# Group norm statistics of the second batch taken inside the front stage instead of in the setup

## The reference, cut to what matters

```
def _gn(v, G=32, eps=1e-5):              # groups of 16 channels, over a whole batch
    g = v.reshape(B_, 32, 16, H_, W_)
    m = mean(g, axis=(2, 3, 4)); s = var(g, axis=(2, 3, 4))
    return (g - m) / sqrt(s + eps)

x = x + mamba_layer(_gn(x), ...)         # layer 0: per position a layer norm over the 512
                                         # channels, in_proj to 2048, a causal conv of 4 taps,
                                         # silu, x_proj, softplus, a selective scan, out_proj
x = x + codebook(_gn(x), m)              # layer 1: 1024 codes
```

## Time and profile before

| | |
|---|---|
| median of 3 runs | 4932.2 us (4929.79 to 4934.46) |
| profiled execution | 4925.77 us, its span 4924.1 us |
| PE busy | 4649.7 us (94% of the span) |
| DVE busy | 4135.4 us (84%) |
| POOL busy | 3377.7 us (69%) |
| ACT busy | 2971.5 us (60%) |
| setup, until the first chunk's load is issued | 0 to 66.4 us |
| group_params and preparation of chunk 0 | 66.4 to 95.3 us |
| front, 16 chunks | about 95 to 1130 us |

### The profile page before, as it was taken

How to read it: one execution, slowest core, us unless ns; L and a number is a source line. 1 busy time by engine, 2 the same in 40 slices (tenths; PEclk the granted TensorE clock), 3 DMA queues, 4 the chain that set the end, 5 groups by cost and what they waited for, 6 DMA issues and landing times. The chain is left out here.

```text
span 4924.1 us, 120048 instructions
## 1 busy us (share of the span) xinstructions
PE 4649.7 (94%) x47160; PEld 2945.8 (60%) x47160; DVE 4135.4 (84%) x4348; ACT 2971.5 (60%) x6008; POOL 3377.7 (69%) x1680
## 2 busy tenths in 40 slices
PE   4999999995899999999999999999999899999999
PEld 4666666663455555555555555555554688887787
DVE  7888898887999999999999999999997676776332
ACT  1666666665777767767777777777765454454111
POOL 0577776775999999999999999999997222222000
PEclk9999999997999999999999999999999999999999
DMA  5344334334223332333233323332332111111453
GB/s 201 120 154 150 141 134 150 142 145 163 85 77 96 96 97 79 96 97 96 79 96 99 98 84 96 95 98 79 96 98 76 44 76 77 77 77 75 190 201 139
DMA packets 191786, 538.37 MB, mean 109 GB/s; under 512 B 15824, under 2 KB 15840, under 8 KB 181840
## 3 DMA queue, kind: packets, MB, share of 16 engines
q1 hardware_dynamic: 185920, 480.31, 29.0%
q0 software_dynamic: 5104, 51.35, 2.7%
q10 hardware_dynamic: 288, 0.00, 0.0%
HBM read 329.22 MB, written 202.38 MB: 108 GB/s over the span
## 5 line engine op out<-in xcount | busy, mean ns | idle before, releaser
L975 POOL TENSOR_TENSOR sc_hc<-sc_hc,sc_c_rep 128x1024 f32<-128x1024 f32 x1024 | 2397.4, 2369 | 191.8 <-ACT sc_state L988 189.3
L1176 DVE TENSOR_TENSOR_SCAN sc_hc<-l_m,sc_state,sc_ring 128x512 f32<-128x512 f32 x2048 | 2432.0, 1259 | 32.5 <-PE sc_ring L1099 27.4
L1020 ACT ACTIVATE l_m<-l1s_v,l_neg_a 128x512 f32<-128x512 f32 x2048 | 1351.8, 707 | 2.5 <-issue 1.5
L1099 PEld LDWEIGHTS sc_ring<-sc_diag,l1s_iota 64*64 64x64 f32 x32768 | 890.6, 133 | 703.2 <-issue 703.2
L1099 PE MATMUL sc_ring<-sc_diag,l1s_iota 64*64 64x128 f32 x32768 | 1102.6, 275 | 8.0 <-DVE sc_hc L1176 5.7
L1109 PE MATMUL sc_y_ps<-sc_hc,sc_fold 128*64 128x512 f32 x4096 | 1008.4, 614 | 27.2 <-POOL sc_hc L975 20.9
L988 ACT ACTIVATE sc_state<-sc_hc 128x2 f32<-128x2 f32 x1024 | 206.0, 201 | 647.1 <-DVE sc_hc L1176 647.1
L851 PE MATMUL sc_o_ps<-l1s_et,l_sums 128*128 128x512 f32 x1024 | 560.6, 634 | 8.7 <-ACT l_count L841 8.7
L1431 POOL TENSOR_TENSOR l_count<-l_count,as_oh 128x1024 f32<-128x1024 f32 x64 | 182.4, 2851 | 506.9 <-DVE as_oh L1614 506.9
L1109 PEld LDWEIGHTS sc_y_ps<-sc_hc,sc_fold 128*64 128x64 f32 x4096 | 251.5, 137 | 415.9 <-issue 381.3
L71 PE MATMUL fr_mm<-fr_xn_hi,l0f_w_in_hi 128*128 128x512 f32 x1024 | 436.9, 427 | 26.3 <-DVE fr_delta L675 11.8
(11 more groups left out here) (172 smaller groups left out, 6518.4 us busy)
## 6 DMA issues: line engine op xcount, KB each, us to landing
sc_duz<-spill SPq DMA_DIRECT2D x128, 768.0 KB, 6.0
l1s_v<-spill SPq DMA_DIRECT2D x256, 256.0 KB, 3.9
spill<-fr_z SPq DMA_DIRECT2D x64, 512.0 KB, 2.8
spill<-fr_u SPq DMA_DIRECT2D x32, 1024.0 KB, 8.7
spill<-fr_du SPq DMA_DIRECT2D x32, 1024.0 KB, 4.3
spill<-fr_delta SPq DMA_DIRECT2D x32, 1024.0 KB, 6.4
sc_c_rep<-bc SPq DMA_DIRECT2D x128, 256.0 KB, 4.3
soft<-l1s_et SPq DMA_DIRECT2D x16, 2048.0 KB, 6.2
```

The source lines that it names most:

```text
L975: nc.gpsimd.tensor_tensor(hc[:, p], hc[:, p], c_rep[:, 2 * q:2 * q + 2, :], ALU.mult).then_inc(s_hp, 1)
L1020: nc.scalar.activation(da[:, p % 4, r, :], delta[:, i % 2, p % 2, :], ACT.Exp, scale=keep.neg_a[:, c:c + 1]).then_inc(s_da, 1)
L1099: done = nc.tensor.matmul(to[:, :, k::4], dut[rows, i % 2, k, HALF * h:HALF * h + HALF], diag[rows, u, 4 * q + c:4 * q + 4:2, k, :], start ...
L1176: nc.vector.tensor_tensor_scan(hc[:, p, r, :], da[:, p % 4, r, :], ring[:, SLOT[at], r::2], state[:, i, 2 * p + r:2 * p + r + 1], ALU.mult ...
```

## The change

`setup` loads and takes the statistics of the first batch's four tiles only (32 `bn_stats`). The weights come in two DMAs with a semaphore each; `lnw` and `lnb` are loaded by SP ahead of them. `group_params` between setup and front handles 4 columns instead of 8 (after the scan it handles 8 as before).

The second batch's 32 `bn_stats` run in chunks 0 to 6 of the front: SP loads a 1 MB chunk of x of the second batch into `sq`, once `sq` is free, and DVE takes 4 `bn_stats`, twice in chunk 0 (before conv 5 and before conv 7) and once in each of chunks 1 to 6 (before conv 7). In chunk 7, before the first chunk of the second batch is normalised, DVE aggregates (at the start of the chunk), PE does the two small matmuls (behind x1 and behind z1), ACT the Sqrt (behind its silu of z1), and DVE the operations between and the scale and shift (behind `rounded`, before `norm_v`).

```diff
@@ group_params
-    n = NB * KC
+    n = stats.shape[1]
@@ setup
         @block.sync
-            sp.dma_start(wf[:], d.w_in).then_inc(weights, 16)
-            with sp.Fori(0, NB * KC // 4) as i:
-                for s in range(4):
-                    sp.wait_ge(stats_done, 4 * i + s + 1)
-                    sp.dma_start(xt[:, s, :], x_rows[4 * i + s]).then_inc(x_tile[s], 16)
+            sp.dma_start(lnw[:], d.ln_w).then_inc(norm_w, 16)
+            sp.dma_start(lnb[:], d.ln_b).then_inc(norm_w, 16)
+            for k in range(2):
+                sp.dma_start(wf[:, 2 * k:2 * k + 2, :], d.w_in[:, 2 * k:2 * k + 2, :]).then_inc(weights[k], 16)
+            for k in range(KC):
+                sp.dma_start(xt[:, k, :], x_rows[k]).then_inc(x_tile[k], 16)
         @block.scalar
-            act.dma_start(lnw[:], d.ln_w).then_inc(norm_w, 16)
-            act.dma_start(lnb[:], d.ln_b).then_inc(norm_w, 16)
             act.wait_ge(norm_w, 32)
-            act.wait_ge(weights, 16)
             for k in range(KC):
+                act.wait_ge(weights[k // 2], 16)
...
         @block.tensor
-            pe.wait_ge(weights, 16)
+            for k in range(2):
+                pe.wait_ge(weights[k], 16)
         @block.vector
-            with dve.Fori(0, NB * KC // 4) as i:
-                for s in range(4):
-                    dve.wait_ge(x_tile[s], 16 * i + 16)
-                    for j in range(NJ):
-                        last = nc.vector.bn_stats(keep.stats[:, 4 * i + s, j, :], xt[:, s, j * T:(j + 1) * T])
-                    last.then_inc(stats_done, 1)
+            for k in range(KC):
+                dve.wait_ge(x_tile[k], 16)
+                for j in range(NJ):
+                    nc.vector.bn_stats(keep.stats[:, k, j, :], xt[:, k, j * T:(j + 1) * T]).then_inc(stats_done, 1)
+            dve.wait_ge(stats_done, KC * NJ)
@@ front, SP
+            def load_next_batch(j):
+                sp.dma_start(sq[:], x_view[1, j]).then_inc(s_xs, 16)
                 if not first:
                     store_delta(g - 1, 0)
+                if b == 0 and after(1)[0] == 0:
+                    sp.wait_ge(s_pre, 2 * g + 4)
+                    load_next_batch(0 if first else j + 1)
                 store_u(g, 0)
                 store_z(g, 2)
+                if first:
+                    sp.wait_ge(s_bn, KC)
+                    load_next_batch(1)
                 store_z(g, 3)
@@ front, ACT
+            def group_root():
+                act.wait_ge(s_gm, 2)
+                nc.scalar.activation(std[:], st_ps[:, KC:2 * KC], ACT.Sqrt, bias=keep.gn_eps[:, 0:1]).then_inc(s_gs, 1)
                 silu_z(g, 1)
+                if after(1) and ends:
+                    group_root()
                 keep_x(g, 2, ends)
...
+                if b == 0 and not first:
+                    act.wait_ge(s_bn, KC * (g + 1))
                 if after(1):
                     square(g + 1)
@@ front, PE
+            def group_mean(g):
+                pe.wait_ge(s_bn, KC * NJ + KC + 1)
+                pe.wait_ge(s_rs, g + 2)
+                nc.tensor.matmul(st_ps[:, 0:KC], keep.gavg[:], mean_v[:], start=True, stop=True).then_inc(s_gm, 1)
+            def group_var():
+                pe.wait_ge(s_bn, KC * NJ + KC + 4)
+                nc.tensor.matmul(st_ps[:, KC:2 * KC], keep.gavg[:], mean_v[:], start=True, stop=True).then_inc(s_gm, 1)
                 project(g, "x", 1, first)
+                if after(1) and after(1)[0] != b:
+                    group_mean(g)
                 project(g, "z", 1, first)
+                if after(1) and after(1)[0] != b:
+                    group_var()
@@ front, DVE
+            def next_batch(j):
+                dve.wait_ge(s_xs, 16 * j + 16)
+                for k in range(KC):
+                    nc.vector.bn_stats(keep.stats[:, KC + k, j, :], sq[:, k, :]).then_inc(s_bn, 1)
+            def group_means():        # 4 bn_aggr, a copy of the means
...
+            def group_spread():       # waits for group_mean; dev = mean - group mean, squared, + variance
...
+            def group_scale():        # waits for group_root; reciprocal, then shift
...
             def main(b, j, after, first):
+                ends = after(1) and after(1)[0] != b
+                if ends:
+                    group_means()
...
                     rounded(g - 1, 0)
+                if ends:
+                    group_spread()
+                    group_scale()
                 if after(1):
                     norm_v(after(1)[0], g + 1)
...
                     invert(g + 1)
+                if first:
+                    next_batch(0)
                 conv(g, 5)
                 if after(1):
                     normalise(g + 1)
                 conv(g, 6)
+                if b == 0 and not ends:
+                    next_batch(1 if first else j + 1)
                 conv(g, 7)
```

More of the change, by code:

```diff
@@ L113, in _ @@
             dve.wait_ge(std_done, 1)
-            nc.vector.reciprocal(scale[:], std[:]).then_inc(step, 1)
+            nc.vector.reciprocal(scale, std[:]).then_inc(step, 1)
             dve.wait_ge(step, n + 5)
-            nc.vector.scalar_tensor_tensor(shift[:], ps[:, 0, 0:n], -1.0, scale[:], ALU.mult, ALU.mult).then_inc(step, 1)
+            nc.vector.scalar_tensor_tensor(shift, ps[:, 0, 0:n], -1.0, scale, ALU.mult, ALU.mult).then_inc(step, 1)
             dve.wait_ge(step, n + 6)
@@ L142, in setup @@
         consts = w.sem("consts")
-        weights = w.sem("weights")
+        weights = [w.sem(f"weights{k}") for k in range(2)]
         x_tile = [w.sem(f"x_tile{i}") for i in range(4)]
-        eps_set = w.sem("eps_set")
         stats_done = w.sem("stats_done")
         bias_done = w.sem("bias_done")
-        exp_done = w.sem("exp_done")
         high = w.sem("high")
@@ L174, in _ @@
         def _(act):
-            act.dma_start(lnw[:], d.ln_w).then_inc(norm_w, 16)
-            act.dma_start(lnb[:], d.ln_b).then_inc(norm_w, 16)
             act.wait_ge(norm_w, 32)
-            act.wait_ge(weights, 16)
             for k in range(KC):
+                act.wait_ge(weights[k // 2], 16)
                 nc.scalar.activation(keep.w_in[0][:, k, :], wf[:, k, :], ACT.Copy, scale=lnw[:, k:k + 1]).then_inc(high, 1)
             act.wait_ge(consts, 16 * n_const)
-            nc.scalar.activation(alog[:], alog[:], ACT.Exp).then_inc(exp_done, 1)
+            nc.scalar.activation(alog[:], alog[:], ACT.Exp).then_inc(high, 1)
         @block.tensor
@@ L195, in _ @@
         def _(dve):
-            nc.vector.memset(keep.gn_eps[:], GN_EPS).then_inc(eps_set, 1)
-            nc.vector.memset(keep.mean_w[:], 1.0 / DIM).then_inc(eps_set, 1)
-            dve.sem_inc(stats_done, 4)
+            nc.vector.memset(keep.gn_eps[:], GN_EPS).then_inc(rest, 1)
+            nc.vector.memset(keep.mean_w[:], 1.0 / DIM).then_inc(rest, 1)
             dve.wait_ge(norm_w, 32)
@@ L253, in front @@
         none = w.sb("none", [P, HIST])
+        mv = w.sb("mv", [P, KC, 2])
+        mean_v = w.sb("mean_v", [P, KC])
+        dev = w.sb("dev", [P, KC])
+        std = w.sb("std", [P, KC])
         mm = w.ps("mm", [P, RING, T])
@@ L259, in front @@
         s_x = keep.x_loaded
+        s_xs = w.sem("next_batch_loaded")
+        s_bn = w.sem("next_batch_taken")
+        s_gm = w.sem("group_summed")
+        s_gs = w.sem("group_std")
         s_v = w.sem("v_done")
@@ L701, in give_delta @@
                 nc.vector.tensor_tensor(du[:, rows, :], u[:, rows, :], delta[:, rows, :], ALU.mult).then_inc(s_du, 4)
+            def next_batch(j):
[3 more added lines that the diff above has]
+            def group_means():
+                dve.wait_ge(s_bn, KC * NJ)
+                for k in range(KC):
+                    nc.vector.bn_aggr(mv[:, k, :], keep.stats[:, KC + k, :, :]).then_inc(s_bn, 1)
+                dve.wait_ge(s_bn, KC * NJ + KC)
+                nc.vector.tensor_copy(mean_v[:], mv[:, :, 0]).then_inc(s_bn, 1)
+            def group_spread():
+                dve.wait_ge(s_gm, 1)
+                nc.vector.tensor_tensor(dev[:], mean_v[:], st_ps[:, 0:KC], ALU.subtract).then_inc(s_bn, 1)
+                dve.wait_ge(s_bn, KC * NJ + KC + 2)
+                nc.vector.tensor_tensor(dev[:], dev[:], dev[:], ALU.mult).then_inc(s_bn, 1)
+                dve.wait_ge(s_bn, KC * NJ + KC + 3)
+                nc.vector.tensor_tensor(mean_v[:], dev[:], mv[:, :, 1], ALU.add).then_inc(s_bn, 1)
+            def group_scale():
+                scale, shift = keep.scale[:, KC:], keep.shift[:, KC:]
+                dve.wait_ge(s_gs, 1)
+                nc.vector.reciprocal(scale, std[:]).then_inc(s_bn, 1)
+                dve.wait_ge(s_bn, KC * NJ + KC + 5)
+                nc.vector.scalar_tensor_tensor(shift, st_ps[:, 0:KC], -1.0, scale, ALU.mult, ALU.mult).then_inc(s_bn, 1)
+                dve.wait_ge(s_bn, KC * NJ + KC + 6)
             def main(b, j, after, first):
                 g = b * NJ + j
+                ends = after(1) and after(1)[0] != b
+                if ends:
```

(6 more changed lines are left out.)

5 lines of the change are left out of this document (2 added, 3 removed).

## The result

The changed kernel took 4903.02 us (median of 7 runs, 4893.75 to 4911.98) against 4929.79 for the kernel before beside it (7 runs, 4919.51 to 4934.46): ratio 0.9946, 95% interval 0.9935 to 0.9958. Measured again in another session it was 0.9960 (0.9947 to 0.9974). Over all sessions the means are 4924.6 us (77 runs of the kernel before, those of e1 not among them; standard deviation of a single run 5.9 us, standard error of the mean 0.7) and 4902.8 us (12 runs, 1.3): 21.8 us faster. By the means, against the kernel before that ran beside it, it was 26.0 us faster the first time and 18.5 the second. Forecast were 16.7 us and 4915.5 us, with a range of 4908 to 4930.

The account below looks back on a forecast made before the run. DVE's 64 `bn_stats` bound setup; POOL and the loop behind it set the front's chunk period. Gain 22.2, less 0.7, 0.5 and 4.3, is 16.7 us: 4932.2 - 16.7 = 4915.5 us, range 4908 to 4930.

Parts of the forecast that it names:

- the base: Whole kernel before: median 4932.2 us, 6.4 us over the profiled execution of 4925.77, a difference taken to stay.
- chunks 1 to 6: Front turns: 2.4 us of `bn_stats` before conv 7 in each, mostly covered by POOL; 0.5 us lost for the six together.
- chunk 7: Last front chunk of the first batch: `norm_v` 6.5 us later through the group step; 4.3 us lost, ends 2 and 7.5.
- chunk 0: First front chunk: two batches of `bn_stats`, 4.8 us on DVE, no POOL work covering the turn; 0.7 us lost.
- Setup and group_params: Before the front: 21.8 us gained in setup and 0.4 in `group_params`, together 22.2 us.
- The wait that ends it: End of setup: fourth x tile lands at 39.1, its `bn_stats` end at 43.9 us; then the chunk load becomes the wait.
- the cover: Chunk turns: DVE's extra work before conv 7 hides behind POOL's `du[7]`; rival without it 4930.6 us, chance 0.16.
- even a gain of 1: Favourable end for chunks 1 to 6: POOL no longer slowed by casts beside its last block; 1 us gained.
- the rule that the prediction took from there: `bn_stats` beside POOL: a DVE instruction with at most one SBUF input, outside two-port modes, doesn't contend with GpSimd.
- POOL's second half: In chunk 7: would be taken at about 588.4 instead of 584.23, 4.2 us later.

Follow-up runs that it names:

- e1: The kernel before, unchanged, timed and profiled once more: ratio 1.0004, mean of 11 runs 4927.2 us.
- e8: The changed kernel with the weights in one load again: ratio 0.9955 to the kernel before, mean 4900.4 us of 6 runs.
- e6: The changed kernel with each of the 32 `bn_stats` of chunks 0 to 6 taken twice: ratio 0.9984 to the kernel before, mean 4916.3 us.
- e2: Only the setup part of the change; no second-batch statistics and no group step in chunk 7: ratio 0.9961 to the kernel before.
- e4: Changed kernel without the loads and `bn_stats` of chunks 0 to 6, keeping setup part and group step: ratio 0.9959 to the kernel before, mean 4905.4 us.
- e13: The setup part of the change alone, measured once more: ratio 0.9956 to the kernel before, mean of these 5 runs 4901.1 us.
- e10: Changed kernel with chunk 7's group step early and PE's `mean` behind z2 and dt 4 to 7: ratio 0.9963 to the kernel before, mean 4903.4 us.
- e15: The changed kernel with the `bn_stats` of chunks 0 to 6 behind conv 7 instead of before it: ratio 0.9959 to the kernel before, mean 4905.0 us.
- e9: The changed kernel with PE's `mean` of chunk 7 behind z2 and dt 4 to 7: ratio 0.9965 to the kernel before, mean 4906.0 us.
- e14: Changed kernel with chunk 7's group step early and ACT's Sqrt before the abs of dt 0 to 3: ratio 0.9955 to the kernel before, mean 4899.4 us.

## Why the prediction was wrong

What failed in the prediction are four terms of the sum: the base, which alone is 7.6 of the 12.5 us; chunks 1 to 6, wrong in sign; chunk 7, too small; and, by less, chunk 0. The 4.1 us that chunks 1 to 6 gave beyond the forecast and the 3.6 that chunk 7 took beyond it nearly cancel, which is luck.

**The base.** The time forecast was 12.5 us above what was measured, and over half of that is no step of the kernel: I let 4932.2, the median of three runs, stand for the kernel before and took the 6.4 us to the profiled execution as a constant. The mean of 77 runs is 4924.6. Three runs that spread by 6 us each don't fix a base to 3 us, and the profiled execution, 4925.77, was the better one. From it the same sum gives 4909.1, still 6.1 us above what was measured. The low end of the range, 4908, stood for 21 to 24 us gained; the gain by the means, 21.8, lies within that, so it is the base that put the time outside.

**Setup and group_params: right, on the profile that it was read from.** 22.2 forecast, 21.6 in the profile (95.4 to 73.8), and setup only gains 21.2 by the means. The wait that ends it is the fourth tile, and then `v`, as said. The early half of the weights is worth some 2 us (e8). What the forecast left out is that the setup before isn't the same length each time: with `lnb` landed 3.4 us later in e1, the first projection came at 98.8. The change loads `lnb` ahead of everything, and with it the first projection came between 72.9 and 73.8 us in 14 profiles, all but that of e8. From the mean of the two profiles before, 97.1, that is 23.8 us; two executions don't fix this mean.

**Chunk 0: a little high.** 0.7 lost forecast; chunk 0 took 55.4 us against 55.9, but over all profiles save e6's it is 55.6 us with the `bn_stats` and 55.7 without: nothing lost.

**Chunks 1 to 6: the sign was wrong.** Forecast 0.5 lost. The nine profiles with the `bn_stats` before conv 7 have a mean of 390.2 us (386.2 to 393.9), the five without (before twice, e2, e4, e13) 393.8 (389.8 to 395.4): 3.6 us gained, with an error of some 1.2. The `bn_stats` are hidden in most turns, as the earlier trace rows said, and e6 shows where the cover ends; in 4 of these 54 turns (three in e8, one in e10) DVE reached the casts 2.0 us behind POOL's last instruction, and there the cover was missing. What I priced at "even a gain of 1" is this. POOL's work of a chunk lasts 49.5 us from its first to its last instruction when the casts start 6.0 us before its end, and 49.25 when they start 3.4 us before it. The rest goes with how DVE's `normalise` meets POOL. These rows of the kernel before, in chunks 2 and 3, show both kinds:

```profile
265.82 2.28 DVE L643 TENSOR_TENSOR l0f_v<-l0f_v,fr_rs 128x2048 f32<-128x2048 f32 x1
332.52 3.18 DVE L643 TENSOR_TENSOR l0f_v<-l0f_v,fr_rs 128x2048 f32<-128x2048 f32 x1
...
265.89 3.37 POOL L388 TENSOR_TENSOR fr_du<-fr_u,fr_delta 128x512 f32<-128x512 f32 x1
333.63 3.22 POOL L383 TENSOR_TENSOR fr_du<-fr_du,fr_e 128x512 f32<-128x512 f32 x1
```

In the first DVE starts 0.07 us ahead of a POOL instruction, which then takes 3.37 us instead of 1.3. In the second DVE starts beside a running one, takes 0.9 us longer itself, and POOL's next takes 3.22 us. So POOL has one instruction stretched by 2 us in both kinds, and still its work of the chunk is 0.8 us shorter in the second without the `bn_stats` (48.7 us against 49.5) and 0.6 with them (48.6 against 49.2); the difference is spread over other instructions and not traced to one. The second kind (`normalise` above 3 us) came in 5 of 30 chunks without the `bn_stats` and in 30 of 60 with them (e15 among these), but unevenly: in none to three of six without, in one to five with. POOL's span fell from 49.4 to 48.9 on average: 2.6 of the 3.6 us. That the second kind is more frequent with the `bn_stats` is counted; why it is, and how it shortens POOL's work, is not shown. The Trainium skill, SBUF — State Buffer, section Who interferes with whom, says that a DVE instruction with two SBUF inputs contends with a GpSimd instruction that reads SBUF, and that the order of issue decides who is blocked. Both kinds agree with that. `bn_stats`, with one SBUF input, runs unslowed at 0.6 us each beside POOL, which agrees with the rule that the prediction took from there.

**Chunk 7: the mechanism was right, the size not.** Forecast 4.3, measured 7.4 in the first pair of profiles and 7.9 over all that have the group step unchanged (seven, 72.3) and not at all (six, 64.4). It was PE's line behind `mean` that set the end, as the prediction had it. The prediction made PE 6.5 us late and gave 2.7 back at the end (606.8 and 614.0 us, from 600.27 and 610.18). Measured in the first pair, `mean` starts 7.4 us later into the chunk (26.85 against 19.41): 5.6 from the late start, where 6.5 was forecast, and 1.9 because `norm_v` itself takes longer beside POOL. From there to x3 PE takes 9.3 us instead of 6.5, with z2 in 5.6 us instead of 3.4 at PE's lower level. That makes 10.3, of which 2.9 come back at `project_x`, where the wait for POOL's last block is gone. The failed step is that the delay was carried through unchanged: the longer `norm_v` and the slow stretch behind PE's wait, 4.7 us together, weren't in the sum. POOL's second half, forecast 4.2 us later, started 6.3 later and still ended before PE. Moving PE's wait alone hardly cut the delay (e9, 1.1 us); an early enough start took it away (e14).

**The sum.** 23.8 in setup, 0.1 in chunk 0, 3.6 gained and 7.9 lost make 19.6 us; the means say 21.8 with an error of 1.5. With the first pair's 21.6 in setup it would be 17.4. So 2 to 4 us stay open. By the means the `bn_stats` give 7.7 (error 2.9) where the stages show 3.6, and the group step costs 7.1 (2.5) with them and 2.0 (2.9) without where they show 7.9; the last is two errors off, the others less. A part of the group step's price may be given back: chunk 8 took 63.2 to 65.0 us behind a long chunk 7, and 64.7 to 67.6 otherwise. But chunks 8 to 14 as a whole scatter from 449.8 to 462.7 us and don't show it, and the scan stage's two lengths, 2661 to 2663 and 2667 to 2671 us, appear in kernels of every kind. This is argued, not shown.

## What to carry to other kernels

Work moved off a path is free where the trace shows two things: another engine that ends later at that place, and operands that have landed by then; moved 9 us earlier, the same four instructions cost everything the change had gained. A serial step costs what stands behind it in each engine's order, and it can reach the engine that ends last by more than one way: taking away PE's longest wait (e9) brought the next one to light and gained 1.1 us, starting the step earlier (e14) gained all. Such a delay also grows on its way, here by an instruction that now ran beside POOL and by PE's lower clock behind its wait. Before a forecast in tenths of a per cent, fix the base by more than three runs, and look at a second profile of the kernel before: a wait of 1.12 us in one was 4.53 in the other.

## What the runs showed of the hardware

- `bn_stats` of 128x512 takes 0.595 us in a row, and 4 of them 2.46 us beside a busy POOL: it isn't held up by it. Four casts of the same size take 1.43 us alone and 4.92 beside POOL.
- A 1 MB load that queues behind 2 MB of stores lands 10.5 us after its issue; with less ahead of it, in chunk 0, 5.4 and 6.1.
- The small load of `lnb`, issued at 1.3 us beside 4 MB of weights and the x tiles, landed at 16.5 us in one execution of the kernel before and at 19.8 in another.
- The table load for a single Sqrt took 1.28 us, and the Sqrt began 1.30 us behind its start.
- PE's granted clock was 0.55 over the 5.5 us behind a wait of 9.17 us, its lower level (1.2 GHz) for most of them, and 1.00 further on in the chunk.
